# Two-layer graph network on one core: a whole step of lag from the start, start-up work in the order of arrival, and rows of two neighbouring blocks interleaved

## What is computed

```python
def L0(input, A, h0, y):                     # masked mean over neighbours of one class
    adj = A * (y @ y.T)
    adj = adj / maximum(sum(abs(adj), axis=1), 1e-12)
    return 0.9 * (adj @ input) + 0.1 * h0

def L1(h, adj, simlar, W_proj, b_proj, W_gcn, b_gcn):
    sim = tanh(adj * simlar)                 # simlar is adj here
    filt = sim * (adj > 0)
    new_adj = the 350 largest of each row of filt
    h2 = tanh(h @ W_proj + b_proj)
    return relu(new_adj @ (h2 @ W_gcn) + b_gcn)

x = layernorm(x + L0(x, adj, h0, y))
x = layernorm(x + L1(x, adj, adj, W_proj, b_proj, W_gcn, b_gcn))
```

## Time and profile before

| | us |
|---|---|
| median of 3 runs | 486.84 |
| lowest, highest | 486.09, 487.06 |
| the profiled execution | 485.75 |
| its span, first to last instruction | 484.0 |
| TensorE busy in the span | 456.3 |
| VectorE, ScalarE, GpSimd busy | 380.0, 262.4, 162.0 |

### The profile page before, as it was taken

The page is one execution under the profiler, slowest core; times in us unless marked ns, Lnnn a source line. Parts: engine busy times, 40 slices in busy tenths (PEclk is TensorE's granted clock), DMA queues, the critical chain, the costliest instruction groups (busy, mean ns, idle before and its releaser), DMA issues.

```text
span 484.0 us, 15414 instructions
## 1 busy us (share of the span) xinstructions
PE 456.3 (94%) x5186; PEld 397.6 (82%) x5186; DVE 380.0 (79%) x1401; ACT 262.4 (54%) x353; POOL 162.0 (33%) x309
## 2 busy tenths in 40 slices
PE   4789998999999999999999999999999999999991
PEld 4567787888889889889888887888888888888881
DVE  3789999999999999999999966656656655665662
ACT  2869888898999999999999934500000000000000
POOL 3022443445645554444444431222122122212210
PEclk8688999999999999999999999999999999999997
DMA  8998999999999999999999200000000000000000
GB/s 238 379 385 311 409 415 395 369 363 399 412 415 421 420 420 418 419 421 419 420 422 420 61 1 1 12 18 11 16 16 15 13 16 16 11 16 16 11 16 15
DMA packets 33090, 108.55 MB, mean 224 GB/s; under 512 B 7801, under 2 KB 23058, under 8 KB 23058
## 3 DMA queue, kind: packets, MB, share of 16 engines
q1 hardware_dynamic: 33058, 108.14, 56.9%
HBM read 105.57 MB, written 2.56 MB: 223 GB/s over the span
## 4 chain that ended last, share of the span: by engine, by line
PE 75%; DVE 12%; ACT 4%; issue 4%; DMA 3%; DVEq 0%; SPq 0%; POOLq 0%; POOL 0%; ACTq 0%
PE acc L485 63%; PE words L435 6%; DVE a_bits L748 4%; DVE turned L833 3%; ACT count_out L650 3%; PE proj_acc L573 2%; DMA a_rows<-in_adj_dram 2%; DMA y_nat<-in_L_gnn_y_dram 2%; PE feat_acc L552 2%; PE xnt_acc L544 1%; ACT x_parts L636 1%; DVE z_high L880 1%; DVE z L887 1%; DVE same_class L853 1%; DVE stats L893 1%
## 5 line engine op out<-in xcount | busy, mean ns | idle before, releaser
L485 PE MATMUL acc<-x_parts,turned 128*128 128x257 f16 (+1 forms) x1600 | 193.9, 275 | 4.2 <-DVE turned L833 4.1
L650 ACT ACTIVATE count_out<-a_rows,ones 128x2560 bf16<-128x2560 f32 (+1 forms) x80 | 189.9, 2374 | 0.5
L485 PEld LDWEIGHTS acc<-x_parts,turned 128*128 128x128 fp8e4 (+1 forms) x1600 | 155.2, 98 | 29.9 <-issue 6.6
L485 PE MATMUL acc<-f_parts,turned 128*128 128x257 f16 (+1 forms) x1560 | 175.4, 273 | 0.0
L485 PEld LDWEIGHTS acc<-f_parts,turned 128*128 128x128 fp8e4 (+1 forms) x1560 | 151.3, 97 | 23.2 <-issue 0.4
L748 DVE TENSOR_SCALAR a_bits<-a_rows 128x2560 bf16<-128x2560 f32 (+1 forms) x80 | 116.6, 1459 | 4.8 <-DMA a_rows<-in_adj_dram 3.6
L833 DVE TENSOR_SCALAR turned<-a_words 128x320 uint16 (+1 forms) x305 | 66.9, 233 | 58.8 <-PE acc L485 58.7
L386 POOL TENSOR_TENSOR var_eps<-mean_var,consts 128x1 f32<-128x1 f32 x80 | 28.5, 356 | 236.5 <-DVE mean_var L1057 143.1
L389 POOL TENSOR_TENSOR rstd<-var_eps,consts 128x1 f32<-128x1 f32 x80 | 81.8, 1022 | 6.3
L833 DVE TENSOR_SCALAR turned<-same_class 128x320 uint16<-128x320 uint16 x313 | 64.2, 249 | 0.5
L435 PEld LDWEIGHTS words<-pack,a_bits 128*128 128x128 bf16 (+1 forms) x1600 | 53.3, 95 | 6.6 <-DVE a_bits L748 2.7
(11 more groups left out here) (113 smaller groups left out, 304.9 us busy)
## 6 DMA issues: line engine op xcount, KB each, us to landing
a_rows<-in_adj_dram SPq DMA_DIRECT2D x39, 1280.0 KB, 8.3
a_rows<-in_adj_dram SPq DMA_DIRECT2D x39, 1220.0 KB, 8.7
h_rows<-in_L_gnn_h_dram SPq DMA_DIRECT2D x39, 64.0 KB, 6.3
out_dram<-xn SPq DMA_DIRECT2D x39, 64.0 KB, 1.5
xs<-in_x_dram SPq DMA_DIRECT2D x3, 640.0 KB, 8.3
xs<-in_x_dram SPq DMA_DIRECT2D x1, 576.0 KB, 7.7
y_nat<-in_L_gnn_y_dram SPq DMA_DIRECT2D x1, 312.0 KB, 8.0
a_rows<-in_adj_dram SPq DMA_DIRECT2D x1, 80.0 KB
```

What stands on the lines that cost most here:

```text
L485: mm = pe.matmul(acc[par][0:m, 0:PARTS], bits, parts[:, b, 0:PARTS], start=first and b == blocks[0], stop=last and b == blocks[-1])
L650: act.activation(count_out[0:m, 0:w], a_rows[par][h][0:m, 0:w], ACT.Relu, bias=ones[0:m, 0:1], scale=-HUGE, accum_out=col).then_inc(s_coun ...
```

## The change

1. **Lag.** `ahead` and `SWITCH` go. From step 3 on TensorE's and VectorE's steps are those that stood from step 17 on: products of block t-2, unpacks spread. Step 2 has no products at all on TensorE (block 1's come in step 3). The unrolled part is 13 steps (`FIRST`), not 17.
2. **Lists in order of arrival.** SyncE issues y first, then the rows of block 0, then x. VectorE casts the rows of block 0 after the y work and splits x after the first unpack. ScalarE copies the words of block 0 before it splits x, and copies the last same-class words of step 1 behind both counts.
3. **Interleaved rows.** Blocks 1 to 38 go in pairs: the first block of a pair has the even rows of 256, the second the odd ones. So the two rows of x or y that a partition holds in neighbouring blocks are neighbours in memory: pieces of 128 B for y (64 B before) and 1 KB for x (512 B before). Rows of `adj`, `h0` and the output are taken with every second row. The packing reads every 2nd column of `a_bits`.
4. **Halves.** The halves have 21 and 19 blocks of columns (2688 and 2312), since a pair must not be cut.
5. **`keep_busy` goes** (82 products).

```diff
-    HB = (NB + 1) // 2
+    HB = NB // 2 + 1
-    SWITCH = 16
+    FIRST = 13
...
+    def rows_in(a, b, par, pair, cols):
+        if isinstance(b, int) and b == LAST:
+            return a[FULL * P:N, cols]
+        if isinstance(b, int) and b == 0:
+            return a[0:P, cols]
+        v = a[P:FULL * P, cols].rearrange("(s p e) c -> e s p c", p=P, e=2)[(par + 1) % 2]
...
+    def column(b):
+        return b * P if b in (0, LAST) else P + (b - 1) // 2 * 2 * P + (b - 1) % 2
+    def spacing(b):
+        return 1 if b in (0, LAST) else 2
...
-        X_PART = [slice(q * NB // 4, (q + 1) * NB // 4) for q in range(4)]
+        X_PART = [slice(q * (NB // 4) + (q > 0), min((q + 1) * (NB // 4) + 1, NB)) for q in range(4)]
...
+        def pairs_of(a, lo, hi):
+            return a[lo * P:hi * P, :].rearrange("(s p e) f -> p s (e f)", p=P, e=2)
...
-            load_half(0, 0, 0)
-            sp.dma_start(y_nat[:, 0:FULL, :], block_view(y)).then_inc(s_in["y"], 16)
+            sp.dma_start(pair_view(y_nat, 1, FULL), pairs_of(y, 1, FULL)).then_inc(s_in["y"], 16)
+            sp.dma_start(y_nat[:, 0, :], y[0:P, :]).then_inc(s_in["y"], 16)
...
-            load_half(0, 0, 1)
+            load_rows(0, 0, 0)
+            sp.dma_start(xs[:, 0, :], x[0:P, :]).then_inc(s_in["x0"], 16)
...
-            keep_busy(36, acc[0])
...
-                    c = b * P - HALF[h].start
+                    c, d = column(b) - HALF[h].start, spacing(b)
                     mm = pe.matmul(words[par][0:k, b * WORDS:(b + 1) * WORDS],
-                                   a_bits[h][0:m, c:c + k], pack[0:m, :], start=True, stop=True)
+                                   a_bits[h][0:m, c:c + (k - 1) * d + 1:d], pack[0:m, :], start=True, stop=True)
...
-            keep_busy(6, acc[0])
...
-                ahead = isinstance(t, int) and t <= SWITCH
+                started = not isinstance(t, int) or t > 2
...
-                if ahead and t == 1:
+                if not started and t == 1:
                     products(0, 0, 0)
                     products(0, 0, 1)
-                elif ahead and t == 2:
-                    products(1, 1, 0)
-                elif ahead:
-                    products(t - 2, par, 1)
-                else:
+                elif started:
                     products(t - 2, par, 0)
...
-                if ahead and 3 <= t < SWITCH:
-                    products(t - 1, odd, 0)
-                elif not ahead:
+                if started:
                     products(t - 2, par, 1)
...
-            cast(0, 0, 0, 0)
-            dve.wait_ge(s_in["y"], 16)
+            dve.wait_ge(s_in["y"], 32)
...
-            cast(0, 0, 0, 1)
+            cast(0, 0, 0, 0)
```

More of the change, by code:

```diff
@@ L340, in store @@
                 sp.wait_ge(s_result, t + 1)
-                sp.dma_start(out[row_range(t, m), :], xn[par][0:m, :]).then_inc(s_out[par], 16)
+                sp.dma_start(rows_in(out, t, par, pair, slice(0, F)), xn[par][0:m, :]).then_inc(s_out[par], 16)
             steps(sp, store, 0)
@@ L415, in _ @@
         def _(pe):
-            def keep_busy(n, bank):
-                for _ in range(n):
-                    pe.matmul(bank[:, NB * WORDS:NB * WORDS + P], ident_b[:, :], ident_b[:, :], start=True, stop=True)
             pe.wait_ge(s_const, 4)
             pe.wait_ge(s_cleared, 2)
-            keep_busy(36, acc[0])
             def pack_rows(t, par, m, h):
@@ L561, in step @@
                     pack_rows(t, par, rows_of(t), 1)
-                if ahead and t == 0:
-                    keep_busy(20, words[1])
+                if isinstance(t, int) and t == 0:
                     for g in range(GRAMS, 2 * GRAMS):
                         gram_words(g)
-                if ahead and t == 1:
-                    keep_busy(20, words[0])
                 if valid(t - 5):
@@ L592, in bias @@
                     .then_inc(s_bias, 1)
-            steps(pe, step, LAG, {2: bias}, SWITCH + 1)
+            steps(pe, step, LAG, {2: bias}, FIRST)
             pe.wait_ge(s_flow, NB)
@@ L614, in _ @@
             act.wait_ge(s_cleared, 2)
[L616 removed]
+            act.wait_ge(s_in["y"], 32)
             act.wait_ge(s_in["yt"], 16)
@@ L705, in step @@
                     count_zeros(t, par, pair, 1, rows_of(t))
+                if isinstance(t, int) and t == 1:
+                    for g in range(2 * GRAMS, 3 * GRAMS):
+                        if not gram_on_dve(g):
+                            copy_words(g)
                 if valid(t - 6):
```

128 lines of the change are left out of this document (51 added, 77 removed).

## The result

| | before | after |
|---|---|---|
| median of 6 runs, us | 486.46 | 478.36 |
| lowest, highest | 485.50, 488.07 | 477.68, 479.46 |
| the profiled execution, its span | 485.75, 484.0 | 478.80, 477.0 |

The ratio is 0.9834, with a 95% interval of 0.9819 to 0.985: the changed kernel is 8.1 us faster. The prediction said 478.5. The two profiled executions differ by 6.95 us.

A forecast was written before the change was run, and what follows sets the result against it. TensorE was taken as the bound from step 17 on, by 1% over the DMA and 3% over VectorE. Step 17 at 35.3 + 88.7 + 2.5 = 126.5 against 134.85 gave 486.84 - 8.35 = 478.5 us, range 475.5 to 484.8.

The forecast's parts named there:

- y first: Start-up: y ahead of the rows, in larger pieces; y work starts at 5.2 us, not 9.33, first pair at 9.9.
- Start-up lists: VectorE's chain from 9.9 us: block 0's products at 19.3 instead of 24.65, TensorE's step 3 at 35.3.
- Clock: Without filler, block 1's products start at the half clock; price 2.5 us, between 1.8 and 4.1.
- Steps 3 to 16: TensorE's work in these steps sums to 88.7 us; nothing added for VectorE, 1 us if its cover were gone.
- a sign of being wrong: Early steps: the prediction is wrong if TensorE waits there for VectorE's unpacks or casts.
- The short lag was what held the early steps: Before, 6.76 us a step against 6.31 later; the rival that it was not: 484.0 us, chance 0.11.
- Step 17: TensorE begins it at 126.5 us against 134.85, 8.35 earlier; the end stands at a fixed distance from there.
- x in larger pieces, priced at nothing: Start-up transfer of x in 1 KB pieces: 6.1 us instead of 7.4, hidden, so taken as 0.
- Every 2nd column, priced at nothing: TensorE's packing: strided weight loads stay hidden, 0 taken; rival at twice the pitch 40 us more, 518 us, chance 0.11.
- Rows at twice the distance: DMA loads of adj: nothing taken; rival of a 5% slower DMA costs 9 us, 487.6 us, chance 0.05.
- The filler: TensorE's filler products stood in its gaps, so taking them out frees nothing.
- The rival that its absence holds the clock down longer: Block 0's and block 1's products wholly at half clock: 3.2 us more, 481.7 us, chance 0.09.

The follow-up runs named there:

- e3: Changed kernel with contiguous rows again: y in 64 B pieces, x in 512 B, packing of every column; order, lag and halves as changed: 480.73 us.
- e5: The changed kernel itself run once more, beside other variants on one chip: 478.22 us.
- e1: Kernel before with only the late steps' lists (whole step of lag) on TensorE and VectorE from step 3 on: 482.86 us, ratio 0.9933.
- e6: Changed kernel with the old short lag in steps 2 to 16, everything else as changed: 483.48 us, ratio 0.9941 to the kernel before.
- e12: Changed kernel, rows still interleaved, but y loaded in 64 B and x in 512 B pieces, each load issued as two: 480.61 us.
- e4: Changed kernel with the packing reading neighbouring columns of a_bits, rows still interleaved; output not the reference's: 479.02 us.
- e11: Changed kernel with packing columns read at a step of 20 (first half) and 18 (second half) instead of 2; output not the reference's: 529.41 us.
- e7: Changed kernel with the four old keep_busy fillers back at their places (36, 6, 20 and 20 products): 479.80 us.

## Why the prediction was right, and where it wasn't

- **y first.** Taken 5.2 for the start of the y work, measured 5.69; first pair 9.9, measured 10.30. y had landed by 4.84. The prediction named GpSimd's constants as what may be late next, "by tenths"; they were, by 0.8. Its assumption that a piece costs the same whatever its size failed: y came at 153 GB/s in 128 B pieces and at 112 in 64 B ones (2 to 4 us, here and in e3), not at twice the rate, and landed some 0.95 us sooner than in e3 (ScalarE's first read at 4.84 and 5.79), not 1.15.
- **Start-up lists.** Block 0's products at 19.3, measured 19.96 and 7.50 us long (7.0 taken); first cast of block 1 at 24.1, measured 24.50. Each later point inherits the 0.4 and adds a tenth or two. Step 3 at 35.3, measured 36.80 (36.33 in e5): 1.5 too early, of which 0.66 stood at block 0's start already, 0.5 is its products and 0.3 what follows them.
- **Clock.** Taken 2.5 in step 3, measured 1.34 in this trace, 2.5 in e5, and 1.3 to 2.6 in the seven traces with this order, without filler or with the old one. The price is right in size and varies, because the clock rises at another point of the step in each execution.
- **Steps 3 to 16.** 88.7 with a full clock in the sum. Measured 90.38 less 1.34, so 89.0. The early steps are as taken: 5.84, 6.28, then 6.5, but 6.95 in step 8, 0.4 more, where I added nothing. In step 7 VectorE had waited for rows:

```profile
62.63 1.56 DVE L746 TENSOR_SCALAR a_bits<-a_rows 128x2688 bf16<-128x2688 f32 x1 [1.08 <-DMA a_rows<-in_adj_dram]
```

The check of y's sums follows in step 8, and TensorE's packing at 71.78 waits for the cast, by 0.18 us. It is the only wait for VectorE from step 3 to 16, and of the kind that the prediction named as a sign of being wrong; it is too small for that. e5 has no such loss in step 8 (6.49), but 0.4 us in step 16 (6.71), with casts that wait 0.41 and 0.77 us for rows ahead of it. The short lag was what held the early steps: e1 and e6 show it from both sides. The support that the prediction gave it, a low DMA rate from 80 to 100 us because of waiting for buffers, was a wrong reading, as said above.
- **Step 17.** 126.5 predicted, 127.18 measured, 7.67 us ahead of before and not 8.35. The medians differ by 8.1. A late start (1.5) and a cheap clock (1.2) offset each other in this trace; in e5, where the clock cost what was taken, step 17 begins at 127.71, 1.2 later than predicted. The mechanism and the size are right; that the median came within 0.2 us of the forecast is luck.
- **x in larger pieces, priced at nothing.** This term failed. It asked only whether x is wanted late, and not what SyncE has queued behind x. The term is worth 2.3 us (e3, e12). The sum was right without it because the start was computed as if rows were always there; with 1 KB pieces no cast waits for rows in the first 60 us of this trace, and one does by 0.57 us in e5 (36.05).
- **Every 2nd column, priced at nothing.** Right (e4), but the reason given, that a slower load has several to hide behind, is wrong: in e11 the loads grew by 64 ns and nothing was hidden. What keeps the cost at zero is that the load isn't slower at a step of 2.
- **Rows at twice the distance.** Nothing, as taken: 0.18 us of waiting in a steady step.
- **The filler.** "Stood in TensorE's gaps and frees nothing" fits the kernel before, where block 0's products waited for VectorE's split of x (23.17 to 24.65 us) and not for the pairs behind the filler; no run took the filler out of that kernel. In the changed one the gaps had closed and it would have cost 1.4 to 1.6 us (e7). The rival that its absence holds the clock down longer fell: with the filler back step 3 takes 7.18 us as without it, and the mean granted clock is no higher (0.967 to 0.971 against 0.980 to 0.985). Block 0's products are no measure of it; without filler they take 5.90 to 7.50 us from one trace to another.

## What to carry to other kernels

Price a transfer by what is queued behind it on its issuing engine, not only by when its own data is wanted; when a start-up has become short, the same piece size that was free before sets it. Two edits that each remove the wait which the other would run into can be worth more together than apart, so a part that measures little alone may still belong. Filler for the clock helped here only in a gap, and gave little back, since rows were late once the clock was up; look at what the next engine waits for before counting its gain.
